# Layer 0's experts on gathered rows of the chosen pairs, after a routing of all batches

## The chip, the cores and the metric

One core of one Trainium2 chip runs the whole program in one launch. The metric is the device time of an execution in microseconds (us), the median of 3 runs. The engines are TensorE (PE in the profile; PEld is its weight load), VectorE (DVE), ScalarE (ACT), GpSimd (POOL) and SyncE (SP), which here only issues DMAs. Each runs its own queue in order and waits for the others by semaphores.

## The reference

Two transformer layers on x of shape (4, 512, 256). Each adds an attention part and a mixture of 8 experts, top 2, both on the layernorm of the same x:

```python
xn = _layernorm(x)
# L0 attention: q, k with rotary cos/sin, v; 16 heads of 16
memory = einsum('bhsd,bhse->bhde', elu(k) + 1, v)        # and softmax attention beside it
# L0 experts (F = 176)
top_w, sel = top_k(xn @ gate_w.T, 2); top_w = softmax(top_w)
h = silu(xn @ gate_proj[e].T) * (xn @ up_proj[e].T)      # for every expert e
out = sum_e tw[:, e] * (h @ down_proj[e].T)              # tw is zero but for the two chosen
x = x + attention + out
# L1: chunked linear attention with decay, experts with H = 512, top 2, the same way
```

## The kernel before

The program has three stages with a barrier between them. Stage one (`layer0_front`, tensors `a_...`) does layernorm, routing, the q/k/v projections, the memory matrix and the experts of layer 0. Stage two (`middle`, `b_...`) does the softmax attention of layer 0, and beside it, one batch behind, everything token-wise up to the routing of layer 1. Stage three (`layer1_main`, `d_...`) does the linear attention and the experts of layer 1; these already work on gathered rows.

Batches are 512 tokens. Matmuls on split operands stand in the helper `three` (L58 to L60): each product is hi x hi, hi x lo and lo x hi, so three matmuls.

In stage one the experts are computed **dense**: all 8 experts' hidden columns (8 x 176 = 1408) lie as 11 tiles of 128, and each tile is computed for all 512 tokens of a batch: `tile` on PE (L624) makes gate and up, 12 matmuls of 512 columns, into `psG`; ACT takes silu (L452), DVE multiplies by up (L528) and by the routing weight of its expert and token (L533, read from `cbc`, which SP loads as broadcast rows), ACT and POOL split the product in hi and lo (L455, L402), and `down` (L637) adds 12 matmuls of 256 columns into `psO`. There are 4 x 11 = 44 tiles. The front part of the next batch (layernorm, transposes, logits, routing, q/k projection with rotation, v, features, memory) stands as steps between the tiles, at places that a dictionary `steps` of every engine gives; PE runs two tiles ahead of `down` (`FAHEAD = 2`). The experts' sum is added to `xacc` in one DVE instruction a batch (L602).

In stage two the inner unit is a slot: four score matmuls, four more for row maxima of a later group (reduced by DVE, L1180), four exponentials on ACT (L1090), four value matmuls. Sixteen slots make a batch; the first batch has no token-wise work beside it. SP sends the maxima through memory (`send_max`, L918, L920) before a group of four slots may begin. At the end the tokens are ranked by expert (L1312 to L1377), which gives `put`, `take` and `expert`, the tables of stage three.

In stage three a block is 128 rows of one expert: POOL gathers them by an indirect DMA (L1767), PE transposes them, computes gate, up and down with the weights of the expert whose number PE loads into a register (`value_load`), and POOL scatters the result (L1776). There are `BLOCKS = 2*2048/128 + 7 = 39` blocks. At the end 32 DVE instructions multiply the returned rows by their weight and add them (L1901).

## Time and profile before

| | |
|---|---|
| median of 3 runs | 1087.56 us (1086.49 to 1091.96) |
| profiled execution | 1091.52 us, its span 1089.6 us |
| PE busy | 946.9 us (87% of the span) |
| DVE / ACT / POOL busy | 588.4 / 433.1 / 314.5 us |
| stage one, two, three (from the stretches' borders) | 299.4, 444.1, 346.1 us |

The span runs from the first to the last instruction; the execution has 1.9 us around it. Busy is time in which an engine works on an instruction; PE's matmuls are pipelined, so one that shows 0.39 us long is followed by the next after 0.23 us, and the distance of the starts is its price in a full queue. The end of stage one is the first instruction of stage two, 299.43 us.

### The profile page before, as it was taken

Reading aid. Unit: us, or ns where it says so; the run is one execution under the profiler, and the core shown is the slowest. Engines: PE = TensorE matmul, PEld = TensorE weight load, DVE = VectorE, ACT = ScalarE, POOL = GpSimd, SP = SyncE. Lnnn points to the kernel's source line nnn. Section 1 sums busy time; section 2 is a strip of 40 time slices with the busy share of each in tenths; the row PEclk is TensorE's granted clock in tenths of the full one; section 3 lists DMA queues with packets and bytes.
Section 4 is the critical chain, followed back from the end, with each engine's and each line's share of the span. In section 5 each row is a group of like instructions: output and inputs, shape, how many; then the busy total and the mean of one; then the engine's idle time right before and its main releaser. Section 6 shows DMA issues by size and latency. Waiting matters only on the chain. (4 is left out here: it accounts for less than half of the span.)

```text
span 1089.6 us, 16172 instructions
## 1 busy us (share of the span) xinstructions
PE 946.9 (87%) x5323; PEld 614.9 (56%) x5323; DVE 588.4 (54%) x1218; ACT 433.1 (40%) x663; POOL 314.5 (29%) x218
## 2 busy tenths in 40 slices
PE   3789999999858999998999988575999999999991
PEld 2678888888711234453445445463666666666660
DVE  4556655563268767647755741474443443443435
ACT  3335536353234554674576467041222222222220
POOL 3632515225233000211021020143333433433321
PEclk9999999999957989888998988786999999999995
DMA  5622414033051221133233112628873433433316
GB/s 200 217 96 60 165 58 144 19 97 126 1 166 58 92 79 60 59 107 131 92 101 118 55 59 99 161 106 298 241 234 86 122 104 88 118 106 97 98 43 236
DMA packets 149836, 125.26 MB, mean 115 GB/s; under 512 B 63232, under 2 KB 127504, under 8 KB 149776
## 3 DMA queue, kind: packets, MB, share of 16 engines
q1 hardware_dynamic: 146032, 114.25, 33.9%
q0 software_dynamic: 3744, 10.23, 2.7%
q8 instruction: 35, 0.57, 0.2%
q14 instruction: 25, 0.20, 0.1%
HBM read 85.56 MB, written 38.86 MB: 114 GB/s over the span
## 5 line engine op out<-in xcount | busy, mean ns | idle before, releaser
L1180 DVE TENSOR_REDUCE b_negmax<-b_psM 128x1 f32<-128x512 f32 x256 | 163.2, 683 | 82.1 <-PE b_psM L1408 79.1
L1090 ACT ACTIVATE b_probs<-b_psE 128x512 f32<-128x512 f32 x256 | 138.8, 595 | 122.8 <-PE b_psE L1426 121.8
L1408 PE MATMUL b_psM<-b_kst,b_qst 96*128 96x512 bf16 x256 | 98.9, 433 | 27.9 <-DVE b_negmax L1180 14.0
L1426 PE MATMUL b_psE<-b_qst,b_kst 98*128 98x512 bf16 x256 | 90.0, 412 | 15.1 <-ACT b_probs L1090 10.5
L402 POOL TENSOR_TENSOR a_hh<-a_h,a_hh 128x512 fp32r<-128x512 f32 x44 | 57.8, 1313 | 144.7 <-ACT a_hh L455 144.7
L1426 PEld LDWEIGHTS b_psE<-b_qst,b_kst 98*128 98x128 bf16 x256 | 21.0, 100 | 109.6 <-ACT b_probs L1090 54.1
L1435 PE MATMUL b_psV<-b_probs,b_vst 128*32 128x512 f32 x512 | 75.9, 667 | 3.1 <-ACT b_probs L1090 3.1
L1928 PE MATMUL d_psG<-d_w,d_xT 128*128 x156 | 76.5, 614 | 2.2 <-DVE d_xT L1827 1.9
L1776 POOL DMA_INDIRECT scratch_ys<-d_y,put x39 | 39.7, 1017 | 129.2 <-ACT d_y L1808 127.8
L1953 PE MATMUL d_psY<-d_w,d_hidden 128*128 x312 | 74.9, 383 | 0.0
L1936 PE MATMUL d_psU<-d_w,d_xT 128*128 x156 | 74.5, 600 | 0.0
L1408 PEld LDWEIGHTS b_psM<-b_kst,b_qst 96*128 96x128 bf16 x256 | 24.3, 100 | 83.6 <-DVE b_negmax L1180 60.1
L1837 DVE TENSOR_TENSOR d_probs<-d_ps,decay 128x512 f32<-128x512 f32 x64 | 43.6, 687 | 47.0 <-PE d_ps L1971 46.9
L528 DVE TENSOR_TENSOR a_h<-a_h,a_psG 128x512 f32<-128x512 f32 x44 | 30.2, 686 | 67.8 <-ACT a_h L452 67.8
L1953 PEld LDWEIGHTS d_psY<-d_w,d_hidden 128*128 128x128 f32 x312 | 57.6, 190 | 12.9 <-issue 6.8
L1808 ACT ACTIVATE d_y<-d_psY 128x256 f32<-128x256 f32 x39 | 14.9, 383 | 122.1 <-PE d_psY L1953 122.1
L1782 POOL TENSOR_TENSOR d_rs<-d_ss,d_neghalf 128x16 f32<-128x16 f32 x16 | 46.9, 2933 | 56.4 <-DVE d_ss L1866 56.4
L1032 POOL TENSOR_TENSOR b_combined<-b_both 128x256 f32<-128x256 f32 x16 | 11.6, 727 | 173.6 <-DVE b_both L1224 173.6
L1832 DVE TENSOR_TENSOR d_hidden<-d_hidden,d_psU 128x512 f32<-128x512 f32 x39 | 26.8, 687 | 59.8 <-PE d_psU L1936 59.8
L1796 ACT ACTIVATE d_hidden<-d_psG 128x512 f32<-128x512 f32 x39 | 23.3, 597 | 85.7 <-PE d_psG L1928 85.7
L455 ACT ACTIVATE a_hh<-a_h 128x512 fp32r<-128x512 f32 x44 | 27.8, 633 | 73.8 <-DVE a_h L533 73.8
L58 PE MATMUL a_psO<-a_wd,a_hh 128*128 128x256 f32 x176 | 50.1, 285 | 1.3 <-POOL a_hh L402 1.3
(314 smaller groups left out, 2125.5 us busy)
## 6 DMA issues: line engine op xcount, KB each, us to landing
scratch_parts<-a_part SPq DMA_DIRECT2D x12, 512.0 KB, 4.3
b_qst<-scratch_parts SPq DMA_DIRECT2D x96, 64.0 KB, 2.1
b_kst<-scratch_parts SPq DMA_DIRECT2D x96, 64.0 KB, 2.1
scratch_parts<-b_part SPq DMA_DIRECT2D x24, 256.0 KB, 3.4
chunk_qst<-scratch_parts SPq DMA_DIRECT2D x96, 64.0 KB, 2.9
chunk_kst<-scratch_parts SPq DMA_DIRECT2D x96, 64.0 KB, 2.2
a_cbc<-scratch_cT SPq DMA_DIRECT2D x16, 256.0 KB, 3.9
scratch_v<-a_v SPq DMA_DIRECT2D x4, 1024.0 KB, 4.4
```

The lines of the kernel that those rows point to most:

```text
L58: nc.tensor.matmul(out, ah, bh, start=start and i == 0, stop=False, skip_group_check=True)
L402: nc.gpsimd.tensor_tensor(hh[s % HSLOTS][1][:, :], h[s % 2][:, :], hh[s % HSLOTS][0][:, :].bitcast(F32), ALU.subtract).then_inc(lo_done, 1)
L1090: nc.scalar.activation(probs[k % PSLOTS][:, h, :], psE[h % 2][:, :], ACT.Exp, scale=float(HD) ** -0.5).then_inc(scores_used[h % 2], 1)
L1180: nc.vector.tensor_reduce(negmax[i][:, t, h:h + 1], psM[:, h % 2, :], AX_X, ALU.max, negate=True).then_inc(rows_used[h % 2], 1)
L1408: nc.tensor.matmul(psM[:, h % 2, :], qst[g][0:STACK, h, t * P:(t + 1) * P], kst[g][0:STACK, h, :], start=True, stop=True).then_inc(rows_re ...
L1426: nc.tensor.matmul(psE[h % 2][:, :], kst[g][0:STACKM, h, k * P:(k + 1) * P], qst[g][0:STACKM, h, :], start=True, stop=True).then_inc(score ...
L1435: mm = nc.tensor.matmul(psV[VW * h:VW * (h + 1), :], vst[g][:, k, VW * h:VW * (h + 1)], probs[k % PSLOTS][:, h, :], start=k == 0, stop=k = ...
L1782: nc.gpsimd.tensor_tensor(rs[:, :], ss[:, :], neghalf[:, :], ALU.pow).then_inc(rs_done, 1)
L1837: nc.vector.tensor_tensor(probs[g][:, :], (ps1 if g % 2 else ps0)[:, :], decay[:, HG * g:HG * g + HG, :].rearrange("p h c -> p (h c)"), AL ...
L1928: mm = nc.tensor.matmul(psG[:, :], xT[b % 2][:, k, :], weights(b, GATE + k * H1, H1), start=k == 0, stop=k == KT - 1)
L1936: mm = nc.tensor.matmul(psU[:, :], xT[b % 2][:, k, :], weights(b, UP + k * H1, H1), start=k == 0, stop=k == KT - 1)
L1953: mm = nc.tensor.matmul(psY[:, 0:D], hT[b % 2][:, k, :], weights(b, DOWN + k * D, D), start=k == 0, stop=k == HT1 - 1)
```

## The change

Stage one is written anew. Its order is a list that every engine walks (`front_order`):

1. The first part of all four batches (`prep`): layernorm, transposes, logits, top-2. The normalised rows are stored to memory (`xn0`). The transposed tokens of all batches stay in SBUF.
2. The ranking of all 4096 (token, expert) pairs: the class `Ranks`, the same operations that stage two has for layer 1, gives `put`, `take` and `expert`. Meanwhile POOL and ACT split the expert weights into hi and lo in 14 pieces (before: 5).
3. 39 blocks of 128 gathered rows. Each has `turn` (2 transposes), `gate` (6 matmuls of 352 columns: gate and up of one expert together), `turn_h` (2 transposes of the 176 hidden columns), `down` (6 matmuls of 256 columns), four ACT and three DVE operations, one gather and one scatter on POOL. The result is not weighted.
4. The projections, features and memory of the attention, in 10 steps a batch (`light`), 40 in all; the first stands before the ranking, the others between the blocks, about one a block.

In stage two, during the first batch of attention, the two returned rows of every token are multiplied by their weights and added: 32 DVE instructions, two a slot (`merge`). SP loads the rows of three batches into the memory of stage three's chunk buffers and those of the fourth when the first are merged.

```diff
+def front_order():
+    prep = [(0, 0), (1, 0), (0, 1), (2, 0), (0, 2), (1, 1), (0, 3), (3, 0), (1, 2), (2, 1), (0, 4), (1, 3), (2, 2), (3, 1),
+            (1, 4), (2, 3), (3, 2), (2, 4), (3, 3)]
+    order = [("prep", n, s) for n, s in prep]
+    lights = [("light", n, s) for n in range(BATCHES) for s in range(10)]
+    order += [lights[0], ("split", 0, 0), ("rank", 0, 0), ("prep", 3, 4), ("invert", 0, 0)]
+    order += [("turn", 0, 0), ("turn", 1, 0), ("gate", 0, 0), ("turn", 2, 0)]
+    rest, given, used = lights[1:], 0, 0
+    for b in range(BLOCKS + 1):
+        for kind, n in (("gate", b + 1), ("turn_h", b), ("down", b - 1), ("turn", b + 3)):
+            if 0 <= n < BLOCKS:
+                order.append((kind, n, 0))
+            used += 1
+            while given < min(len(rest) * used // (4 * (BLOCKS - 3)), len(rest)):
+                order.append(rest[given])
+                given += 1
+    return order
...
 @block.tensor
+            def gate(b, _):
+                owner[b] = pe.value_load(expert[0:1, b:b + 1], min_val=0, max_val=E - 1)
+                pe.wait_ge(xb_lo, b + 1)
...
+                if b >= 2:
+                    pe.wait_ge(mult_done, b - 1)
+                hi, lo = xb[b % 2]
+                pairs = []
+                for k in range(KT):
+                    wh, wl = (w[:, bass.ds(owner[b], 1), k * 2 * F0:(k + 1) * 2 * F0].rearrange("p a n -> p (a n)") for w in wgu)
+                    pairs.append((hi[:, k, :], lo[:, k, :], wh, wl))
+                three(nc, psG[:, b % 2, 0:2 * F0], pairs).then_inc(gate_ps, 1)
+            def turn_h(b, _):
+                pe.wait_ge(mult_done, b + 1)
+                if b:
+                    pe.wait_ge(hT_lo, b)
...
+            def down(b, _):
+                pe.wait_ge(hT_lo, b + 1)
...
+                if b:
+                    pe.wait_ge(y_done, b)
...
+            def light(n, s):
+                if s in (0, 2):
+                    project_qk(n, s // 2)
+                elif s == 4:
+                    project_v(n)
+                elif s == 6:
+                    turn_kf(n)
+                elif s == 8:
+                    memorise(n)
 @block.gpsimd
+            def turn(b, _):
+                if b + XSLOTS < BLOCKS:
+                    gather(b + XSLOTS)
+            def down(b, _):
+                pool.wait_ge(y_done, b + 1)
+                nc.gpsimd.indirect_dma_start(scratch["ys0"], bass.IndirectOffsetOnAxis(ap=put[:, b:b + 1], axis=0),
+                                             y[b % YSLOTS], None).then_inc(put_out[b % YSLOTS], 16)
 @block.scalar
+            def light(n, s):
+                if s == 2:
+                    exp_part(n, 0)
+                    first(n, 0)
+                elif s == 4:
+                    exp_part(n, 1)
+                elif s == 5:
+                    copy_v(n)
+                    first(n, 1)
...
 stage two, SP, before the first attention group
+            for n in range(BATCHES):
+                if n == BATCHES - 1:
+                    sp.wait_ge(merged, 2)
+                for i in range(2):
+                    sp.dma_start(back(n, i), scratch["ys0"][i * TOK + n * SEQ:i * TOK + (n + 1) * SEQ, :]
+                                 .rearrange("(t p) d -> p t d", p=P)).then_inc(back_in[n], 16)
 stage two, DVE, once a slot of the first batch
+            def merge(k):
+                for j in range(2 * k, 2 * k + 2):
+                    n, i, t = j // (2 * TILES), j // TILES % 2, j % TILES
+                    if j % (2 * TILES) == 0:
+                        dve.wait_ge(back_in[n], 32)
...
+                    last = nc.vector.scalar_tensor_tensor(x, back(n, i)[:, t, :], wts0[i][:, n * TILES + t:n * TILES + t + 1], x,
+                                                          ALU.mult, ALU.add)
```

PE between two units of expert work. Before, the end of a tile's `down` (`a_psO`), a step of the next batch and the start of the next tile:

```order
L58 MATMUL a_psO<-a_wd,a_hh 128x256
L59 MATMUL a_psO<-a_wd,a_hh 128x256
L60 MATMUL a_psO<-a_wd,a_hh 128x256
L651 ISA
L652 ISA
L655 MATMUL a_psT<-a_ident,a_xn 128x128 x8
L630 REGISTER_ALU
L58 MATMUL a_psG<-a_xTf,a_wg 128x512
L59 MATMUL a_psG<-a_xTf,a_wg 128x512
L60 MATMUL a_psG<-a_xTf,a_wg 128x512
```

Now the round of block 2 (`a_psH` is the transposed hidden, `a_psY` the block's result, `a_psT` the projection of q and k that stands as a step, `a_psG` the gate of the next block):

```order
L917 MATMUL a_psH<-a_ident,a_h 88x128 x2
L56 ISA
L56 MATMUL a_psY<-a_wd,a_hT 128x256
L57 REGISTER_ALU
...
L894 MATMUL a_psX<-a_ident,a_xg 128x128 x2
L56 MATMUL a_psT<-a_xT,a_wqk 128x512
...
L898 TENSOR_LOAD a_rk_expert
L898 ISA x2
L56 ISA
L56 MATMUL a_psG<-a_wgu,a_xb 128x352
```

The long runs of equal tiles are gone: a unit of expert work is 16 short matmuls and transposes, each with the weights picked by a number that PE loads for that block.

ACT around the exponential of the key and query features (`a_rot`), with the two table loads about it. Before it stands between two tiles of 512 columns (`a_h`, `a_hh`):

```order
L452 ACTIVATE a_h<-a_psG 128x512
L455 ACTIVATE a_hh<-a_h 128x512
L470 ISA
L471 ACT_TABLE_LOAD
L471 ACTIVATE a_rot<-a_rot 128x1024
L478 REGISTER_ALU
L479 ACTIVATE a_part<-a_qk 128x1024
L450 REGISTER_ALU
L452 ACT_TABLE_LOAD
L452 ACTIVATE a_h<-a_psG 128x512
```

Now it stands between a block's copies (`a_y` the result, `a_xb` the gathered rows, `a_hT` the hidden):

```order
L679 ACTIVATE a_hT<-a_psH 88x256
L686 ACTIVATE a_y<-a_psY 128x256
L666 ACTIVATE a_xb<-a_psX 128x256
L691 ACT_TABLE_LOAD
L691 ACTIVATE a_rot<-a_rot 128x1024
L697 ACTIVATE a_part<-a_qk 128x1024
L673 ACT_TABLE_LOAD
L673 ACTIVATE a_h<-a_psG 128x176
```

The step itself is unchanged; what stands before and behind it is a round of smaller instructions.

DVE in the first batch of stage two, a group of four slots. Before:

```order
L1180 TENSOR_REDUCE b_negmax<-b_psM 128x1 x4
L1203 COPY b_nmT<-b_psN 8x512
L1180 TENSOR_REDUCE b_negmax<-b_psM 128x1 x12
L1188 CAST b_nmparts<-b_negmax 128x4x4
L1190 TENSOR_TENSOR b_nmparts<-b_negmax,b_nmparts 128x4x4
L1210 COPY b_outT<-b_psV 128x512
```

Now:

```order
L1453 TENSOR_REDUCE b_negmax<-b_psM 128x1 x4
L1476 COPY b_nmT<-b_psN 8x512
L1680 SCALAR_TENSOR_TENSOR xacc<-held,wts,xacc 128x256 x2
...
L1453 TENSOR_REDUCE b_negmax<-b_psM 128x1 x4
L1680 SCALAR_TENSOR_TENSOR xacc<-held,wts,xacc 128x256 x2
L1461 CAST b_nmparts<-b_negmax 128x4x4
```

Each slot's four reductions are now followed by two merges.

## Rows read from the trace of the kernel before

**Rows 1.** Windows: length; PE, PEld, DVE, ACT, POOL busy (instructions); granted clock; DMA share; GB/s.
```profile
0.00:299.43 299.43, 261.12 (x1488) 227.15 (x1488) 162.31 (x326) 128.25 (x157) 117.82 (x74) 0.98 0.33 108
299.43:743.50 444.07, 372.77 (x1889) 175.85 (x1889) 279.32 (x578) 229.01 (x356) 71.70 (x49) 0.86 0.31 98
743.50:1089.60 346.10, 312.98 (x1946) 211.90 (x1946) 146.77 (x314) 75.88 (x150) 124.98 (x95) 0.95 0.48 143
308.00:331.00 23.00, 19.37 (x37) 3.55 (x36) 21.16 (x36) 9.18 (x25) 4.68 (x3) 0.50 0.58 162
336.00:395.80 59.80, 54.60 (x267) 13.33 (x268) 45.98 (x80) 32.54 (x60) 0.00 (x0) 0.95 0.22 68
```

**Rows 2.** Timeline, PE, inside a tile: start, duration, engine, line, operands, shape.
```profile
77.44 0.39 PE L58 MATMUL a_psG<-a_xTf,a_wg 128*128 128x512 f32 x1
77.67 0.40 PE L59 MATMUL a_psG<-a_xTf,a_wg 128*128 128x512 f32 x1
...
79.65 0.28 PE L59 MATMUL a_psO<-a_wd,a_hh 128*128 128x256 f32 x1
79.77 0.28 PE L60 MATMUL a_psO<-a_wd,a_hh 128*128 128x256 f32 x1
```

**Rows 3.** Timeline, the front part of the first batch, and POOL beside it.
```profile
13.15 1.02 ACT L462 ACTIVATE a_xT<-a_psT 128x1024 fp32r<-128x1024 f32 x1 [4.69 <-PE a_psT L655]
14.21 1.22 DVE L544 TENSOR_TENSOR a_xT<-a_psT,a_xT 128x1024 fp32r<-128x1024 f32 x1 [3.18 <-ACT a_xT L462]
...
17.84 6.12 POOL L433 TENSOR_TENSOR a_wg<-a_cbc,a_wg 128x2816 fp32r<-128x2816 f32 x1 [9.80 <-ACT a_wg L446]
...
20.26 0.35 PE L59 MATMUL a_psT<-a_wv,a_xT 128*128 128x8 f32 x1
20.47 0.35 PE L60 MATMUL a_psT<-a_wv,a_xT 128*128 128x8 f32 x1
...
21.57 2.42 DVE L153 TENSOR_TENSOR a_rt_gap<-a_rt_top 128x4 f32<-128x4 f32 x1
```

**Rows 4.** Timeline, DVE, first and last instruction of the ranking for layer 1.
```profile
716.45 0.15 DVE L1312 COPY b_counts<-b_psE 128x8 f32<-128x8 f32 x1
...
740.50 0.18 DVE L1377 TENSOR_SCALAR take<-put 128x40 uint32<-128x40 uint32 x1
```

**Rows 5.** Timeline, PE, stage three's second transposes and first gate (a register load between).
```profile
754.02 0.41 PE L1915 MATMUL d_psX<-ident,d_xg 128*128 128x128 f32 x2 [1.83 <-DVE d_xT L1827]
755.22 1.22 PE L1928 MATMUL d_psG<-d_w,d_xT 128*128 x1 [0.80 <-DVE d_xT L1827]
```

**Rows 6.** Timeline, POOL, two gathers in a row.
```profile
747.61 0.95 POOL L1767 DMA_INDIRECT d_xg<-scratch_xn,take  x1 [0.30 <-issue]
748.87 0.95 POOL L1767 DMA_INDIRECT d_xg<-scratch_xn,take  x1 [0.30 <-issue]
```

**Rows 7.** DMA issues: out<-in, queue, count, median us to landing.
```profile
d_xg<-scratch_xn,take POOLq DMA_INDIRECT x39, 3.6
```

**Rows 8.** Groups by line, stage one: busy us, mean ns; idle before, releaser.
```profile
L414 POOL TENSOR_TENSOR a_qk<-a_qk,a_part 128x1024 f32<-128x1024 f32 x8 | 19.7, 2457 | 7.6 <-DVE a_rot L583 7.6
L583 DVE SCALAR_TENSOR_TENSOR a_rot<-a_qk,a_rot 128x1024 f32<-128x1024 f32 x8 | 13.3, 1667 | 5.8 <-ACT a_rot L471 5.8
L452 ACT ACT_TABLE_LOAD x10 | 12.8, 1283 | 0.2
L471 ACT ACTIVATE a_rot<-a_rot 128x1024 f32<-128x1024 f32 x8 | 8.5, 1062 | 10.7 <-DVE a_rot L576 10.6
```

**Rows 9.** Timeline, stage two's first batch: ends of the first and fourth group; SP's maxima.
```profile
339.90 0.28 SPq L918 DMA_DIRECT2D scratch_max<-b_nmT  x1
...
351.89 0.69 DVE L1210 COPY b_outT<-b_psV 128x512 f32<-128x512 f32 x1
...
395.81 0.69 DVE L1210 COPY b_outT<-b_psV 128x512 f32<-128x512 f32 x1
```

**Rows 10.** One line's instructions: count, ns min/median/max, first and last start, shape.
```profile
L1901 DVE SCALAR_TENSOR_TENSOR xacc<-d_w,wts,xacc x32: 479/479/485, 1073.0 to 1085.8; 128x256 f32<-128x256 f32 x32
```

More of the change, by code:

```diff
@@ L302, in loop @@
-        def loop(eng, run):
-            with eng.Fori(0, BATCHES - 1) as b:
-                run(b, False)
-            run(BATCHES - 1, True)
-        def tiles(b, last, tile, steps):
-            for t in range(FT0):
-                before, behind = (() if last else steps.get((t, place), ()) for place in range(2))
-                for step in before:
-                    step(b + 1)
-                if not (last and t + FAHEAD >= FT0):
-                    tile(b, t + FAHEAD)
-                yield t
-                for step in behind:
-                    step(b + 1)
@@ L322, in start @@
-        def start(tile, steps):
-            for place in sorted(steps):
-                for step in steps[place]:
-                    step(0)
-            for t in range(FAHEAD if tile else 0):
-                tile(0, t)
-        def run_steps(eng, tile, steps):
-            def run(b, last):
-                for t in tiles(b, last, tile, steps):
-                    pass
-            return run
+        xmem = sb("xg", [P, XSLOTS * D])
+        xg = [xmem[:, i * D:(i + 1) * D] for i in range(XSLOTS)]
@@ L437, in _, with subtract @@
[L437 to L440 removed]
+            def subtract(i):
+                raw, hi, lo = piece(i)
+                pool.wait_ge(w_hi, i + 1)
+                if i:
+                    pool.wait_ge(w_lo, i)
+                nc.gpsimd.tensor_tensor(lo, raw, hi.bitcast(F32), ALU.subtract).then_inc(w_lo, 1)
@@ new lines, in split, with invert @@
+            def split(_, __):
+                for i in range(BATCHES, PIECES):
+                    subtract(i)
+                pool.wait_ge(w_lo, PIECES)
+            def invert(_, __):
+                pool.wait_ge(ranks.put_done, 3)
+                pool.wait_ge(xn_stored, 16 * BATCHES)
+                for b in range(XSLOTS):
+                    gather(b)
+            def turn(b, _):
[5 more added lines that the diff above has]
+                                             y[b % YSLOTS], None).then_inc(put_out[b % YSLOTS], 16)
@@ new lines, in rank, with invert, turn @@
+            def rank(_, __):
+                pe.wait_ge(routing.copied, BATCHES)
+                ranks.count(pe, psL)
+            def invert(_, __):
+                pe.wait_ge(ranks.routed, 12)
+                ranks.turn_over(pe, psL)
+            def turn(b, _):
+                s = b % XSLOTS
+                pe.wait_ge(gathered[s], 16 * (b // XSLOTS + 1))
+                if b == 1:
+                    pe.wait_ge(ranks.put_done, 3)
+                if b >= 2:
+                    pe.wait_ge(xb_lo, b - 1)
+                for k in range(KT):
+                    mm = nc.tensor.transpose(psX[b % 2][:, k * P:(k + 1) * P], xg[s][:, k * P:(k + 1) * P], ident[:, :])
+                mm.then_inc(x_ps, 1)
@@ L705, in memorise @@
                 pe.wait_ge(kf_copied, n + 1)
+                pe.wait_ge(ones, 2)
                 for k in range(KT):
@@ L870, in middle, with loop @@
         SLOTS = GROUPS * TILES
-        def loop(eng, attend, steps, ready=lambda: None):
+        def loop(eng, attend, steps, ready=lambda: None, first=lambda k: None):
             def batch(b, beside, last):
                 for g in range(GROUPS):
-                    attend(b, g, last, lambda k: [step(beside) for step in steps.get(TILES * g + k, ()) if beside is not None])
+                    attend(b, g, last, lambda k: first(TILES * g + k) if beside is None else
+                           [step(beside) for step in steps.get(TILES * g + k, ())])
             batch(0, None, False)
```

892 lines of the change are left out of this document (543 added, 349 removed).

## The prediction

> **What bounds the kernel now.** I read the windows by stage first [rows 1]. Stage one takes 299.43 us with PE busy for 261.12 at a granted clock of 0.98, that is 2.4 GHz nearly throughout, while DVE, ACT and POOL are busy for half of it or less. Stage one is bound by PE. In the first batch of stage two (the stretch from 336) three engines are close together: PE 54.60 and DVE 45.98 of 59.80 us. Then I read the timeline of PE inside a tile, for what a matmul costs in a full queue [rows 2]: 512 columns follow each other after 0.23 us, 256 columns after 0.12. A tile has 12 of either, 2.76 + 1.44 = 4.2 us, and 44 tiles are 185 us of the 299. That is what the change is after. The rest of stage one is the start, before tiles run, and the steps between them.
>
> The sum below is made against the profiled execution, 1091.5 us (span 1089.6). The median of the runs is 1087.6, so I take 4 us off at the end.
>
> **Stage one, up to the first block.** All four batches are routed before any expert runs. In the start of before, a batch passes through 8 transposes, a copy of 1.02 us on ACT, a difference of 1.22 on DVE and 24 small matmuls for the logits; these follow each other after 0.21 us, the clock being at 1.2 GHz there [rows 3]. That is 1.7 + 1.0 + 1.2 + 5.1 = 9.0 us, and as one batch's logits keep PE from the next one's transposes, the four come nearly one after the other. The first batch's logits end at 21 us as before; three more at 9.6 with the waits bring 50, the last top-2 gives 52. On PE the first q/k projection (12 matmuls at 0.43, the 1.2 GHz price of 512 columns) stands before the ranking: 55.5, and 17 counting matmuls: 57.5. The ranking itself is the chain that stage two has for layer 1: from 716.45 to 740.68, 24.2 us [rows 4]. Then a gather, 1.26 to issue [rows 6], 3.6 to landing [rows 7], and two copies: the first block's gate starts at **88 us**.
>
> The ranking's 24.2 us hold waits for POOL. One is in [rows 3]: a DVE instruction on 4 numbers lasts 2.42 us and ends when POOL's subtraction of 6.12 us, which began at 17.84, ends. In the change POOL still has nine or ten pieces to subtract then (6.12 us for 2816 columns, so 1.5 to 2.3 each, some 18 in all), about as much as it was busy beside the old chain. I keep 24; without such waits it would be 15, with more of them 32, so the block phase starts between 78 and 97.
>
> **Stage one, the 39 blocks.** Two floors. PE: a block has 6 matmuls of 352 columns (between 0.12 and 0.23, I take 0.16), 6 of 256 at 0.12 and 4 transposes at 0.12: 2.16 us, 39 times 84. A batch's attention steps are 24 matmuls of 512 columns, 24 of 256 and 16 short ones: 5.5 + 2.9 + 1.9 = 10.3, four times 41, of which 3 came before: 38. Together 122 us. New is a register load before each gate. Its bounds are in [rows 5]: 1.20 us lie between the start of two transposes and the gate behind them, 0.24 of it theirs, so up to 0.96 us where PE has nothing queued, and nothing where it has. I take 0.3, near the lower end since the blocks mostly leave work queued: 12 us (bounds 0 and 37). The Trainium skill gives such a load a floor of about 0.6 us (DMA: Bandwidth & Descriptors, Latency and other measured facts); by that alone, never hidden, it would be 23 us instead of 12.
>
> POOL: a gather and a scatter at 1.26 each [rows 6], 39 times 98 us, and 16 subtractions of the split at 2.46 [rows 8] are 39: 137 us. POOL, not PE, is the higher floor: 3.5 us a block.
>
> Neither floor will be reached, since the queues are in order and a block's chain has only one round of slack (`turn_h` needs the hidden of the gate one round earlier). Before, `FAHEAD` gave two tiles, 8.4 us. The step with the exponential costs ACT a wait of 10.7/8 = 1.3 for DVE, a table load of 1.28, 1.06 for itself, a copy of as much, and 1.28 to load the silu table back [rows 8]: 6.0 us, once a batch, and 4.9 once more without the copy. Against a round of 3.3 that leaves PE 2.7 and 1.6 idle. `turn_kf` waits for a DVE product of the same step (1.67, rows 8) behind the copy of the gathered rows: 2.7. So 7 us a batch, 28 in all. Rounds without a step, and the filling and emptying, cost about 6. Sum: 122 + 12 + 28 + 6 = **168 us**, 4.3 a block. Bounds: 137 (POOL's floor) and 205 (each wait twice as long, and the load never hidden).
>
> The end needs a last scatter and its landing and the barrier, 5 us. Stage two starts at 88 + 168 + 5 = 261 instead of 299.4: **38 us less** (between 8 more and 79 less). The removed row loads of the weights (`cbc`), POOL's 44 subtractions and `L602` were all beside PE and give nothing of their own.
>
> **Stage two.** Two merges a slot are 32 instructions, issued every 12.8/31 = 0.41 us [rows 10]: 13.2 us. A slot of the first batch lasts (395.81 - 351.89)/12 = 3.66 us [rows 9], and DVE idles (59.80 - 45.98)/16.3 = 0.85 us in each [rows 1]. The two merges want 0.83. They fit only if every gap is usable, and part of the gaps is waiting for PE, who in turn waits for the reductions. Between 0 and 13.2 I take 7. What is queued behind the merges are the next reductions, and PE's row matmuls wait for these.
>
> SP now waits for the first two `merged`, at the end of slot four, before it may send the maxima of the second group; before, these left at 339.90, 12 us before they were needed. The next group's scores then start some 4.5 us late (0 to 6). The first merge waits for rows whose load can't leave before the stage begins: 2 us (0 to 4). Together **13 us more** (1 to 24). Stage three is untouched, but for line numbers.
>
> Sum: 1091.5 - 38 + 13 = 1066.5, and for the median 4 less: **1063 us**.
>
> **The rivals.**
> *All hidden but POOL.* ACT's long steps fall into slack and the blocks run at POOL's 137 us: 31 less again, 1032. For it: stage three runs the same block scheme with PE busy 312.98 of 346.10 [rows 1]. Against: its blocks last over 7 us of PE each, so POOL and ACT have twice the slack there.
> *No change.* The block phase takes 193 us (4.95 a block), and start and merges eat the gain: 1083 to 1092. It needs twice my waits.
> *The clock, slower.* PE waits in each round, the clock falls to 1.2 GHz and stays: the 122 us of PE work become 244, the load and the filling stay, 262 us, and the time is 1063 + 94 = 1157; with half of the phase at that clock, 61 more, some 1120. It decides from about 25 us of extra PE time on. For it: in the stretch from 308 to 331, where PE waits for DVE after each pair of matmuls, the granted clock is 0.50. Against it: from 336 on PE waits too, in smaller pieces, and has 0.95 [rows 1]. The Trainium skill has a rule that speaks for it (TensorE: Matmul & The Clock Gate, A second HAM failure mode: psum-queue depth-cycling): frequent short idles between groups of matmuls make the clock swing. I trust the 0.95 more, since a slot of attention is about as long as a block.
>
> **Chances.** Forecast (1048 to 1078) 0.52; all hidden 0.22; no change 0.10; clock 0.16. A measurement of this kernel can tell 0.5%, 5.4 us, from no change. Faster by more: the first two and a little of the third, 0.77; within it 0.06; slower 0.17. The range 1030 to 1108 takes in most of the fast rival and the mild part of the slow one; the forecast's own is 1048 to 1078.
>
> **What would show it.** Right: the first gate of 352 columns at 78 to 97 us; starts of gates 4.3 us apart on average, the longest gaps at the exponentials and before `turn_kf`; stage two's first instruction near 261; slots of the first batch at 4.1 us with a gap once after the fourth; granted clock over 0.85 in the blocks. Wrong: a clock near 0.5 there, gates over 5 us apart, POOL's indirect DMAs much longer than 1 us, or a ranking over 32 us.

## The result, and the profile after

Over six runs each, on the same chips, the changed kernel takes 1079.6 us (median, 1074.2 to 1081.6) and the kernel before 1090.7 (1086.5 to 1095.0): ratio 0.9887, 95% interval 0.9855 to 0.992. It is faster, by 11 us or 1.1%. Forecast were 24.5 us, 2.3%; the time lies inside the range of 1030 to 1108, but the gain is just under half of what was forecast.

The profiled execution took 1074.2 us, 17.3 less than that of before. By stages, from one profile of each (here the border of stage three is its first instruction, 744.05 us before and 726.53 after, so stage two of before is 0.5 us longer than in [rows 1]):

| us | before | forecast | after |
|---|---|---|---|
| first gate of a block | | 88 | 89.2 |
| blocks, first gate to last `down` | | 168 | 176.9 |
| from there to stage two | | 5 | 9.6 |
| stage one | 299.4 | 261 | 275.7 |
| stage two | 444.6 | 457 | 450.9 |
| stage three | 345.6 | unchanged | 345.8 |
| profiled execution | 1091.5 | 1066.5 | 1074.2 |
| median less profiled | | -4 | +5.4 |

The windows by stage, then the block phase, the first batch of stage two, and the rest of it; the columns are those of [rows 1]:

```profile
0.00:275.66 275.66, 182.64 (x1089) 167.40 (x1089) 148.70 (x372) 118.71 (x228) 152.13 (x121) 0.87 0.37 120
275.66:726.53 450.87, 371.00 (x1889) 171.60 (x1889) 290.78 (x610) 229.00 (x356) 71.71 (x49) 0.86 0.34 106
726.53:1072.30 345.77, 313.23 (x1946) 212.00 (x1946) 146.74 (x314) 75.86 (x150) 124.73 (x95) 0.95 0.53 144
89.20:266.10 176.90, 144.42 (x896) 133.70 (x896) 90.58 (x188) 100.47 (x203) 114.27 (x91) 0.89 0.37 126
275.66:387.55 111.89, 82.67 (x311) 18.73 (x312) 82.58 (x150) 45.48 (x91) 17.63 (x12) 0.72 0.41 124
387.55:726.53 338.98, 288.33 (x1580) 152.87 (x1578) 208.20 (x461) 183.52 (x266) 54.08 (x37) 0.90 0.31 99
```

Stage one's granted clock was 0.98 in [rows 1]; in the block phase it is 0.89. PE is busy for 144.4 us there and idle for 32.5. At the pitches of a full queue at 2.4 GHz (the distance from one start to the next) the same matmuls cost 118: 234 gates at 0.16, 234 downs at 0.12, 76 pairs of transposes at 0.14, 84 of 512 columns at 0.23, 96 of 256 at 0.12 and 11 for the rest. So 26 us of "busy" lie above these pitches. Most of them stand in the timeline behind the longest kind of wait (PE; the bracket is the idle time before):

```profile
201.32 0.39 PE L894 MATMUL a_psX<-a_ident,a_xg 128*128 128x128 f32 x2
206.70 1.94 PE L964 MATMUL a_psT<-a_ident,a_rot 128*128 128x128 f32 x8 [4.99 <-DVE a_rot L830]
208.29 0.64 PE L56 MATMUL a_psG<-a_wgu,a_xb 128*128 x1
208.73 0.50 PE L57 MATMUL a_psG<-a_wgu,a_xb 128*128 x1
209.02 0.50 PE L58 MATMUL a_psG<-a_wgu,a_xb 128*128 x1
...
212.33 0.32 PE L57 MATMUL a_psG<-a_wgu,a_xb 128*128 x1
212.49 0.32 PE L58 MATMUL a_psG<-a_wgu,a_xb 128*128 x1
```

Before the wait PE ran at 2.4 GHz; behind five idle microseconds a gate matmul follows the last after 0.29 us, at 212 us after 0.16 again. The granted clock is 0.50 in 37.4 of the 176.9 us. The first 3.3 of them are left from before the phase; the rest are seven stretches, and each begins within a wait of 1.4 to 5.0 us or at most 1.1 us behind one. What the matmuls in all of them cost above the 2.4 GHz pitches is 16 us. The other 10 or 11 us stand at full clock. Some 4 are the matmul before an idle time, whose recorded length is more than its pitch, so a bit of waiting is booked as busy. Some 6 are the first matmul of a group, also in a full queue: the first gate takes 0.25 us instead of 0.16 and the first `down` 0.20 instead of 0.12. The waits themselves (engine, line, what released it: total, times, longest):

```profile
PE a_psT L964 <- DVE a_rot L830: 17.6, 4, 5.0
PE a_psT L56 <- DVE a_rot L815: 10.6, 8, 1.9
PE a_psH L917 <- DVE a_hT L800: 2.8, 4, 1.2
PE a_psY L56 <- ACT a_y L686: 0.9, 2, 0.7
PE a_psG L56 <- issue: 0.7, 2, 0.4
```

The last row would show the register loads before the gates: 0.7 us, where 12 were forecast.

In stage two the answer to [rows 9] is, on SP and DVE:

```profile
312.06 21.57 SPq L1210 DMA_DIRECT2D held<-scratch_ys  x8
333.74 0.34 SPq L1184 DMA_DIRECT2D scratch_max<-b_nmT  x1
337.77 0.26 SPq L1186 DMA_DIRECT2D b_qst<-scratch_max  x1
...
315.97 0.41 DVE L1476 COPY b_nmT<-b_psN 8x512 bf16<-8x512 bf16 x1 [0.75 <-PE b_psN L1707]
319.32 0.88 DVE L1680 SCALAR_TENSOR_TENSOR xacc<-held,wts,xacc 128x256 f32<-128x256 f32 x2 [2.94 <-DMA held<-scratch_ys]
...
332.88 0.68 DVE L1483 COPY b_outT<-b_psV 128x512 f32<-128x512 f32 x1
357.91 0.68 DVE L1483 COPY b_outT<-b_psV 128x512 f32<-128x512 f32 x1
```

The maxima lie ready at 316.4 us and leave at 333.7. Eight row loads stand ahead of them in SP's queue, but their issue takes little: six are out by 316.9, and then SP stands until 332.7, for the second `merged`. From the store of the maxima to SP's next issue it is 4.0 us, where it was 1.3 before (339.90 to 341.19); the last two row loads left right ahead of it and landed at 336.6 and 338.0. PE waits for what the maxima release:

```profile
339.34 1.03 PE L1718 MATMUL b_psE<-b_qst,b_kst 98*128 98x512 bf16 x2 [6.89 <-DMA b_qst<-scratch_max]
```

This wait is paid twice too: from 334.9 to 348.5 us the granted clock is 0.50. It was also 0.50 from 321.2 to 328.0, where the first group's reductions had kept PE idle for 2.0 us. Between the ends of the first and the second group are 25.0 us instead of 14.6; the third and fourth take 14.8 as against 14.6. The first batch costs 111.9 instead of 96.4 us, 15.5 more.

And the end of stage one on POOL, the last scatters and stage two's first instruction:

```profile
265.42 0.97 POOL L608 DMA_INDIRECT scratch_ys<-a_y,a_rk_put  x1 [0.82 <-ACT a_y L686]
267.05 0.97 POOL L608 DMA_INDIRECT scratch_ys<-a_y,a_rk_put  x1 [0.67 <-ACT a_y L686]
275.66 1.80 POOL L1337 MEMSET b_kst<- 2x2048 bf16 x1 [7.64 <-POOLq L72]
```

The scatter has landed 2.4 us after its issue, at 269.5. Then nothing runs and no byte moves for 6 us. Before, stage two began 1.1 us after DVE's last instruction.

### The profile page after: what moved, and what is told of

The parts are those of the page before. It is cut to its first block and busy times, and to the rows that moved or that the text cites. A ratio compares the mean times of both kernels' runs of the same rounds, so it can differ in the third digit from the quotient of the medians.

```text
span 1072.3 us, 15783 instructions
## 1 busy us (share of the span) xinstructions
PE 866.9 (81%) x4924; PEld 551.0 (51%) x4924; DVE 586.2 (55%) x1296; ACT 423.6 (40%) x734; POOL 348.6 (33%) x265
## 5 line engine op out<-in xcount | busy, mean ns | idle before, releaser
L1363 ACT ACTIVATE b_probs<-b_psE 128x512 f32<-128x512 f32 x256 | 138.8, 595 | 130.9 <-PE b_psE L1718 130.3
L1700 PE MATMUL b_psM<-b_kst,b_qst 96*128 96x512 bf16 x256 | 101.8, 443 | 37.5 <-DMA b_vst<-scratch_v 18.2
L608 POOL DMA_INDIRECT scratch_ys<-a_y,a_rk_put x39 | 43.2, 1108 | 43.8 <-ACT a_y L686 38.6
L581 POOL DMA_INDIRECT a_xg<-scratch_xn,a_rk_take x39 | 41.3, 1059 | 27.9 <-issue 19.3
L2057 POOL DMA_INDIRECT d_xg<-scratch_xn,take x39 | 38.1, 977 | 21.4 <-issue 11.0
L2218 PEld LDWEIGHTS d_psG<-d_w,d_xT 128*128 128x128 f32 x156 | 27.3, 194 | 23.2 <-issue 23.1
```

The costliest lines, as they stand in the source:

```text
L581: nc.gpsimd.indirect_dma_start(xg[s], None, scratch["xn0"].rearrange("b s d -> (b s) d"), bass.IndirectOffsetOnAxis(ap=take[:, b:b + 1], a ...
L608: nc.gpsimd.indirect_dma_start(scratch["ys0"], bass.IndirectOffsetOnAxis(ap=put[:, b:b + 1], axis=0), y[b % YSLOTS], None).then_inc(put_ou ...
L1363: nc.scalar.activation(probs[k % PSLOTS][:, h, :], psE[h % 2][:, :], ACT.Exp, scale=float(HD) ** -0.5).then_inc(scores_used[h % 2], 1)
L1700: nc.tensor.matmul(psM[:, h % 2, :], qst[g][0:STACK, h, t * P:(t + 1) * P], kst[g][0:STACK, h, :], start=True, stop=True).then_inc(rows_re ...
L2218: mm = nc.tensor.matmul(psG[:, :], xT[b % 2][:, k, :], weights(b, GATE + k * H1, H1), start=k == 0, stop=k == KT - 1)
```

## The experiments

Ratios are against the kernel before on the same chip. "Blocks" is first gate to last `down`, as in the table.

### Both kernels once more

> The changed kernel once more, for the spread of each stage between two profiles. If the profiled execution of the change (1074.2 us) was only a lucky one, this profile lies at 1077 to 1082 us, and the 3 to 7 us more stand in stage two, whose later three batches took 274 us in the changed kernel and 283 in the kernel before on the same code: then the 8.5 us were chance. If they belong to the change, stage two's later batches take 274 us again and the total stays within 2 us of 1074. Stage one is expected within 3 us of 275.7 by both.

> The kernel before once more, for the spread between two profiles. Stage one 299 us within 1; the later twelve groups of stage two vary in steps of 1.3 to 1.7 us in every profile of the changed kernel (12 groups and the end 331 to 345 us); if that holds for the code of before too, this profile differs from the first by 2 to 8 us there and nowhere else.

The change: 1079.3 us, ratio 0.989 (0.984 to 0.994), this profile 1084.2, above the 1077 to 1082 that I had given it. Blocks 176.8 us, end 9.6, first batch of stage two 112.2: all repeat to 0.3 us. Two runs below whose stage one is untouched have 177.0 (late_rows) and 178.7 (no_merge) for the blocks, so one profile of them is good to some 2 us. What moved is the rest of stage two, 347.0 instead of 339.0. The kernel before, profiled again (1093.5): first batch 96.9, and the rest

```profile
400.60:746.10 345.50, 294.19 (x1581) 159.31 (x1582) 207.43 (x460) 183.86 (x266) 53.52 (x37) 0.88 0.31 97
```

where the first profile had 348.2. Over the 18 profiles of this study this stretch lasts 339.0 to 348.2 us, whatever was edited, and the two profiles first compared are the ends of that range. The 9 us that the change seems to gain there are chance, and more than cover the difference between 17 us by profiles and 11 by medians. That stage one repeats within 3 us held for the change (277.6) but was too narrow for the kernel before (303.7; I had said within 1).

### Stage two: SP's order, and the merges

`late_rows`:

```diff
             load(0, 3)
-            for n in range(BATCHES):
-                if n == BATCHES - 1:
-                    sp.wait_ge(merged, 2)
-                (load the returned rows of batch n)
+            load_back(0)
 in attend, behind send_max:
+                if isinstance(b, int) and b == 0 and g < 3:
+                    if g == 2:
+                        sp.wait_ge(merged, 2)
+                    load_back(g + 1)
```

> SP sends the second group's maxima right after the rows of the first batch; the rows of the second to fourth batch are loaded behind the sends of the next groups. Queue theory (the 21.6 us in which SP's queue issues the row loads and waits for the first merges hold back the maxima, 333.7 us in the changed kernel where they were ready at 316.4): the first four groups of stage two end at 88 to 92 us after its start instead of 96.4 plus 15.5, that is 103 instead of 112, the second group takes 15 us instead of 25, and the time falls by 8 to 11 us. Rival (the merges themselves hold DVE and so PE): the second group stays above 20 us and the time falls by less than 3 us.

1065.0 us, ratio 0.979 (0.974 to 0.984), 1.0% below the change. In time that is 14 us below it on the same chip, where 8 to 11 were expected. On SP the maxima now leave soon:

```profile
313.47 1.06 SPq L1208 DMA_DIRECT2D held<-scratch_ys  x2
317.58 0.29 SPq L1184 DMA_DIRECT2D scratch_max<-b_nmT  x1
319.34 0.26 SPq L1186 DMA_DIRECT2D b_qst<-scratch_max  x1
319.64 0.93 SPq L1208 DMA_DIRECT2D held<-scratch_ys  x2
```

The second group takes 14.8 us, and from 319.8 us to the end of the batch the granted clock is 1.00. The first batch takes 98.3 us. That is 13.6 us less than in the change. I expected 88 to 92 in one place and 103 in another for it; the first was a slip, and the second too cautious, since the first group gained as well (53.8 instead of 57.2).

`no_merge` leaves the row loads and the merges out:

```diff
             def merge(k):
+                return
```

> Leaves out the load of the returned rows and the 32 merges of stage two, so layer 0's experts are not added. It prices all of what stage two pays. Queue theory: the first batch falls back to the 96.4 us of the kernel before, 15 us less, and with late_rows at 10 less, the merges on DVE are worth 5 or less. Rival (merges are dear on DVE, as the prediction's 7 us and its bound of 13.2): this one lies over 8 us below late_rows.

1069.1 us, ratio 0.981. Its first batch takes 96.8 us, as before (96.4). So loads and merges, well placed, cost 98.3 - 96.8 = 1.5 us; the queue order cost 13.6, between these two profiles. The eleven profiles with the change's order of SP have 106.4 to 112.2 us for this batch, whatever was edited in stage one, and the four with the late loads 98.0 to 99.9: the order costs 6.5 to 14 us. The total lies above that of late_rows only by the rest of stage two (348.1 against 343.0).

### The blocks: where PE waits, and what the wait costs

`turn_later`, PE's and ACT's steps on the key features one step later (ACT's copy, from step 7 to 8, is not shown):

```diff
-                elif s == 6:
+                elif s == 7:
                     turn_kf(n)
-                elif s == 8:
+                elif s == 9:
                     memorise(n)
```

> PE transposes the key features one step later (and ACT's copy and PE's memory matmuls too), so DVE's product has a round more. In the changed kernel PE waits 17.6 us in four places for it, and each time its clock is low for some 5 to 10 us behind. Theory that the waits bring the low clock: these four waits shrink under 1.5 us each, the granted clock of the blocks rises from 0.89 to 0.93 or more, and stage one is 14 to 24 us shorter. First rival (the clock falls whatever PE does): the waits go, the clock stays at 0.89, stage one is 10 to 16 us shorter. Second rival (ACT with its table loads and copies is the limit, the wait only moves): stage one less than 5 us shorter, and PE waits as long for ACT's copies of the blocks.

1078.6 us, ratio 0.989: nothing. Blocks 178.6 us. The waits of PE:

```profile
PE a_psT L56 <- DVE a_rot L814: 10.7, 8, 1.9
PE a_psT L971 <- ACT a_xn L716: 8.1, 4, 2.5
PE a_psH L916 <- DVE a_hT L799: 4.7, 6, 1.8
PE a_psT L963 <- DVE a_rot L829: 3.5, 3, 1.7
```

The wait for L829 (L830 in the change) fell from 17.6 to 3.5 us and came back before the memory matmuls and before `turn_h`. The second rival holds in that the wait only moves; that ACT's table loads are behind it is not what exp_as_copy shows below.

`feature_early`, the product itself earlier:

```diff
-                elif s in (5, 6):
-                    feature(n, s - 5)
+                elif s == 5:
+                    feature(n, 0)
+                    feature(n, 1)
```

> DVE makes both feature products one step earlier, behind each other, instead of the second behind the block's work of the next step. In the changed kernel the exponential that it needs ended at 197.7 us, DVE began the product at 204.7 and PE waited until 206.7. Theory that DVE's order makes this wait: the four waits of 4 to 5 us (17.6 together) fall to 2 to 3 each, under 11 together, and the blocks take 7 to 12 us less than 177, a part of it from the clock. Rival (it moves elsewhere, as in turn_later): blocks 174 to 179, with more waits for DVE's other products (L790, L800).

1069.9 us, ratio 0.980 (0.977 to 0.984). The window of the blocks:

```profile
89.70:258.30 168.60, 142.54 (x896) 129.76 (x896) 85.81 (x188) 99.61 (x203) 116.25 (x91) 0.93 0.39 133
```

and PE's wait is down from 17.6 to 7.3:

```profile
PE a_psT L965 <- DVE a_rot L830: 7.3, 4, 2.8
```

The exponential had long been done; what held the product was DVE's own order, as DVE's rows of the change show, where it stands behind the block's differences (L800, L790), which wait for ACT:

```profile
201.99 1.22 DVE L830 SCALAR_TENSOR_TENSOR a_rot<-a_qk,a_rot 128x1024 f32<-128x1024 f32 x1
203.85 0.42 DVE L800 TENSOR_TENSOR a_hT<-a_psH,a_hT 88x256 fp32r<-88x256 f32 x1 [0.65 <-ACT a_hT L679]
204.39 0.42 DVE L790 TENSOR_TENSOR a_xb<-a_psX,a_xb 128x256 fp32r<-128x256 f32 x1
204.73 1.82 DVE L830 SCALAR_TENSOR_TENSOR a_rot<-a_qk,a_rot 128x1024 f32<-128x1024 f32 x1
```

`fill` leaves the waits and gives PE something to do in them:

```diff
                 pe.wait_ge(v_copied, n + 1)
+                for _ in range(32):
+                    nc.tensor.matmul(psT[:, 0, 0:D], wv[0][:, 0, 0:P], xT[n][0][:, 0, 0:D], start=True, stop=True,
+                                     skip_group_check=True)
                 pe.wait_ge(features, 2 * n + 2)
```

> At the four places where PE waits 4 to 5 us for DVE's product it first runs 32 matmuls of 256 columns into a buffer that is free there (3.8 us of work with no use, behind ACT's copy of v, so inside the wait). Nothing else is changed. Theory that PE's waits bring the low clock: the pitches at double length behind these places go, the sum of slow pitches falls from 16 us to 10 or less, the granted clock of the blocks rises to 0.92 or more and the blocks are 4 to 8 us shorter, though PE has 15 us more to do. Rival (the clock falls by itself, or by the sum of the work): slow pitches stay at 14 to 18 us, the blocks take 176 to 180.

1071.9 us, ratio 0.981 (0.978 to 0.984). The block phase, then the same place as above:

```profile
91.00:262.60 171.60, 154.17 (x1024) 141.53 (x1024) 90.63 (x188) 100.42 (x203) 116.10 (x91) 0.95 0.39 130
```

```profile
200.99 4.08 PE L961 MATMUL a_psT<-a_xT,a_wv 128*128 128x256 f32 x32 [0.96 <-ACT a_v L710]
204.97 1.09 PE L967 MATMUL a_psT<-a_ident,a_rot 128*128 128x128 f32 x8
205.84 0.42 PE L56 MATMUL a_psG<-a_wgu,a_xb 128*128 x1
206.10 0.32 PE L57 MATMUL a_psG<-a_wgu,a_xb 128*128 x1
206.26 0.32 PE L58 MATMUL a_psG<-a_wgu,a_xb 128*128 x1
```

With 128 useless matmuls more (15.4 us) the blocks are 5.3 us shorter. Take these 15.4 from PE's 154.2: the useful part took 138.8 instead of 144.4. The eight transposes take 1.09 instead of 1.94 us and the gates follow each other after 0.16 instead of 0.29. So the idle wait brings the low clock here; this is shown. The stretches at a granted clock of 0.50 shrink from 37.4 to 16.7 us, and what the matmuls in them cost above the 2.4 GHz pitches falls from 16 to 7, under the 10 that were set. Three stretches are left; they begin at 107.7, 193.1 and 234.0 us, within or just behind the waits of 1.7 to 1.9 us before the v projections, which were not filled.

`exp_together` and `exp_as_copy`:

```diff
 exp_together, ACT
                 if s == 2:
-                    exp_part(n, 0)
                     first(n, 0)
                 elif s == 4:
+                    exp_part(n, 0)
                     exp_part(n, 1)
 exp_as_copy, ACT
-                nc.scalar.activation(rot[:, half, :], rot[:, half, :], ACT.Exp).then_inc(exp_done, 1)
+                nc.scalar.activation(rot[:, half, :], rot[:, half, :], ACT.Copy).then_inc(exp_done, 1)
```

> Both exponentials of a batch stand in one step, so ACT loads 4 exponential and 4 silu tables less (8 times 1.28 us, 10.2 us of ACT). In turn_later the four waits for DVE's product (17.6 us) came back as 17 us at other places, so ACT's chain is suspected. Theory that ACT's chain of table loads and copies sets these rounds: the blocks take 8 to 12 us less than 177, and the four waits of 4 to 5 us fall under 4. Rival (the wait is the chain PE, DVE, ACT, DVE of a projection, in which a table load is hidden behind DVE's 2.8 us): the blocks stay within 3 us of 177.

> The exponentials of stage one are replaced by copies of the same size: no table is loaded between the blocks (16 loads, 20.5 us of ACT, go; the features are wrong). If ACT's chain sets the rounds: blocks 15 to 22 us shorter, and if the low clock comes from the waits, the granted clock of the blocks rises from 0.89 to 0.93 or more and the pitches at double length (16 us of them) halve. If the chain of a projection sets them: under 5 us, the clock unchanged.

1070.1 us, ratio 0.980 (0.977 to 0.982), blocks 165.7; and 1066.8 us, ratio 0.974, blocks 169.7. The windows of the block phase, first the joined exponentials, then the copies:

```profile
91.50:257.20 165.70, 137.84 (x896) 128.43 (x896) 90.58 (x188) 91.48 (x195) 114.62 (x91) 0.92 0.40 135
```

```profile
89.20:258.90 169.70, 141.57 (x895) 131.34 (x896) 91.41 (x188) 80.05 (x187) 117.38 (x91) 0.90 0.39 132
```

Neither fits its theory. The joined exponentials gained the 11 us, but not where I said: the four long waits stayed (17.7). All of PE's idle time fell by 4.6 us (32.5 to 27.9) and its busy time, on the same matmuls, by 6.6. Without any table load but the first (exp_as_copy) the idle time is the same 28.1, and the blocks are 4 us longer by busy time alone. So a table load as such is mostly hidden, and the two differ by where the clock fell. Why it fell less in the first stays open; in a second profile of the joined form (below) the blocks take 167.1.

`fixed_owner`:

```diff
-                owner[b] = pe.value_load(expert[0:1, b:b + 1], min_val=0, max_val=E - 1)
+                owner[b] = b // 5
```

> Each block's expert number is fixed as block / 5 in the program, so PE loads no register (the wrong weights are used). The prediction held 12 us for these loads; the trace of the changed kernel shows 0.7 us of waits before gates that nothing else explains. By the trace: blocks within 2 us of 177. By the prediction: 12 us less. A third way: the loads delay PE's queue where no wait is shown, at the first matmul behind a wait: 3 to 8 us less.

Blocks 176.3 us against 176.8 to 178.7 in the four profiles of the same stage with the loads: the 39 loads cost 0.5 to 2.4 us together. The ratio (0.985, 0.982 to 0.988) is nominally lower, by stage two's first batch (108.5) and the rest of it.

`lights_last`, the steps of the attention all behind the last block:

```diff
-            while given < min(len(rest) * used // (4 * (BLOCKS - 3)), len(rest)):
+            while False:
...
+    order += rest[given:]
     return order
```

> All attention steps but the first stand behind the last block, so the 39 blocks run alone, and the steps alone after them. PE's work of a block is 2.0 to 2.2 us, POOL's gather and scatter 2.5. If POOL is the floor of a block, as the prediction has it: 2.5 to 2.7 us a block, 98 to 105 in all. If one round of slack is too short for the chain through ACT and DVE: 3 us or more, over 117. If neither, PE sets it: 80 to 88. The steps alone should take over 35 us a batch, 140 in all, so the time is 60 us or more above the changed kernel: the mixing hides them.

1093.6 us. The windows of the blocks alone, then of the steps alone:

```profile
89.80:187.00 97.20, 91.66 (x620) 83.88 (x620) 44.86 (x119) 49.58 (x155) 71.09 (x73) 0.97 0.31 100
187.00:285.80 98.80, 63.23 (x279) 51.87 (x277) 46.68 (x70) 33.48 (x34) 38.46 (x20) 0.79 0.33 120
```

2.49 us a block, where two indirect DMAs at POOL's pitch of 1.26 make 2.52: the price per block that the prediction's floor rests on fits. POOL's idle time there is 18.9 us of "issue", the 0.3 us that lie between any two of its indirect DMAs, and only 7.5 us of waits for others. But PE is busy for 91.7 of the 97.2 us too, at a granted clock of 0.97, where 39 times the prediction's 2.16 is 84; and no third quantity was varied. One round of slack is enough for a block alone. The steps took 98.8 us, not over 140, and the whole took 19 more than the change's profile, in one run, not 60: mixing the two hides only 196 - 177 = 19 us.

### The end of the stage

`tail` spreads the steps so that the last seven stand behind or between the last two blocks, and `pool_end` also gives POOL's last subtraction to DVE:

```diff
-            while given < min(len(rest) * used // (4 * (BLOCKS - 3)), len(rest)):
+            while given < min(len(rest) * used // (4 * (BLOCKS + 5)), len(rest)):
...
+    order += rest[given:]
 pool_end, DVE (and POOL's own step 8 only for n < BATCHES - 1)
+                elif s == 8 and n == BATCHES - 1:
+                    nc.vector.tensor_tensor(parts[2][:, half, :], qk[:, half, :], parts[1][:, half, :], ...)
```

> The attention steps are spread wider, so that the last seven stand behind the last two blocks, and the last scatter leaves some 10 us before the stage ends. In the changed kernel 9.6 us lie between the last matmuls of a block and stage two, 6.6 us of them behind the last bytes of the last scatter; in the kernel before 1.1 us lie between DVE's last instruction and stage two. Theory (POOL's queue takes long after a scatter, before the barrier opens): from the last instruction of any engine to stage two under 3 us. Rival (the barrier itself is longer now, for the many semaphores that it clears or for the code that it loads): 6 us again from the last instruction or store to stage two. The time as a whole may rise by up to 10 us, since the last steps lie bare.

> As tail (last seven attention steps behind the last blocks), and POOL's last subtraction goes to DVE, so that POOL's last instruction ends 3 to 5 us before the last store leaves. In all kernels of this shape stage two starts 7.65 us after POOL's last instruction, whether that is a scatter or a subtraction. If POOL's queue holds the barrier for 7.6 us after its last instruction: stage two starts 7.65 us after POOL's last again, so 3 to 4 us after the last store's issue. If it is the barrier or SP's wait: 7.3 us after the last store's issue again, as in tail, and over 10 us after POOL's last instruction.

tail: 1072.7 us, ratio 0.980 (0.977 to 0.983); stage two starts at 270.2, 5.5 earlier, so the wider spacing gains where I feared a loss. pool_end: 1066.7 us in one run. POOL in tail, then in pool_end:

```profile
260.40 2.12 POOL L622 TENSOR_TENSOR a_part<-a_qk,a_part 128x1024 bf16<-128x1024 f32 x1 [1.17 <-ACT a_part L703]
270.18 3.54 POOL L1338 MEMSET b_kst<- 2x2048 bf16 x2 [7.66 <-POOLq L72]
```

```profile
259.94 2.13 POOL L616 TENSOR_TENSOR a_qk<-a_qk,a_part 128x1024 f32<-128x1024 f32 x1
269.73 1.80 POOL L1344 MEMSET b_kst<- 2x2048 bf16 x1 [7.65 <-POOLq L72]
```

In pool_end the last store leaves 4.9 us before stage two, in tail 7.3; but from the end of POOL's last instruction it is 7.65 in both, as in every kernel here with the new stage one (7.64 to 7.66), whether that instruction is a scatter or a subtraction. POOL holds the barrier. The theory that I gave tail, a POOL that is slow just behind a scatter, fails with it. In the kernel before, whose stage one has no indirect DMA, stage two started 4.15 us after POOL's last instruction, and 1.1 after DVE's. That the indirect DMAs make the difference, and not something else in the new stage, is argued, not shown.

### Together

```diff
 late_rows_exp_together = late_rows + exp_together
 best2 = late_rows + exp_together + feature_early + tail
 best3 = best2 + POOL's last subtraction on DVE + fill with 12 matmuls instead of 32
```

> Both edits that gained by themselves: the late row loads (ratio 0.979 against the kernel before) and the joined exponentials (0.9795), where the change alone has 0.989. One sits in stage two, the other in stage one, so they should add: 1.0 + 1.0 per cent below 0.989, ratio 0.966 to 0.973. Rival (both only shift the phase of the clock in stage two, whose later groups vary by 10 us from run to run): 0.975 to 0.980. Blocks 165 to 167 us, first batch of stage two 98 us.

> late_rows, exp_together, feature_early and tail's wider spacing together. If their gains add in the blocks (11 for the joined exponentials, 6 for the spacing, 8 for the products) and 14 in stage two: stage two starts at 250 to 256 us and the ratio to the kernel before is 0.950 to 0.960. If the waits are shared and count once: stage two at 259 to 264, ratio 0.961 to 0.967, no better than late_rows_exp_together's 0.966.

> best2 with POOL's last subtraction on DVE, and 12 matmuls without use (1.4 us) where PE waits for the products. POOL theory: stage two starts 7.65 us after POOL's last instruction and 2 us or more earlier than in best2. Clock theory: granted clock of the blocks 0.01 to 0.03 higher than in best2. Together 2 to 6 us less than best2; rival: within 2 us of it, since the waits are already short.

Ratios 0.966 (0.963 to 0.970; 1056.6 us), 0.960 (0.957 to 0.963; 1046.2) and 0.956 (0.953 to 0.960; 1042.7 us): each beats both kernels, best3 the kernel before by 4.4%. Stage two starts at 256.8 in best2, a little behind the 250 to 256 of gains that add, and at 251.5 in best3, 7.65 us behind POOL in both; the difference of their ratios is within the intervals. The window of best3's block phase, which has some 24 useful matmuls fewer inside, since these stand behind the last block:

```profile
89.10:235.40 146.30, 133.83 (x908) 123.33 (x908) 85.55 (x186) 85.36 (x191) 104.29 (x87) 0.98 0.39 131
```

Idle time is 14.8 us in best2 and 12.5 in best3, the clock 0.96 and 0.98: less waiting, a higher clock, twice paid.

## Why the prediction was right and wrong, by its steps

**Start.** The first gate of 352 columns was forecast at 88 us and stands at 89.2 (91.2 in the second profile). The ranking takes 26.3 us (56.65 to 82.96), where 24 were taken from stage two of before: that chain, with its waits for POOL, was the right measure.

**PE's work in the blocks, the step that failed.** "Together 122 us" is right as a count of matmuls times their pitch at 2.4 GHz in a full queue (118 by the count above), and it was taken as the time that PE spends. It spent 144.4. Of the 26 us more, 16 are the low clock. The prediction had this mechanism as its rival "the clock, slower", but as a matter of all or half of the phase, and priced the forecast itself at no slow clock at all, on the 0.95 of [rows 1]. The measured clock of 0.89 is 21% of the phase at 1.2 GHz, in pieces behind the waits. The forecast's own 28 us of waits should have carried such a price. The other 10 us were in no rival: units cut this short cost more than count times pitch at full clock too, as the first matmuls of the groups in fill show (205.84 to 206.10 us, 0.26 instead of 0.16). The Trainium skill (TensorE: Matmul & The Clock Gate, A second HAM failure mode: psum-queue depth-cycling), cited for the rival, speaks of frequent short idles between groups of matmuls, with which the clock swings. The trace agrees in kind, with seven falls of the clock in the phase, and fill shows the cause.

**Register loads, over-priced.** 12 us were held; fixed_owner measures 0.5 to 2.4. The row used as bound showed PE with nothing queued, and in the blocks PE mostly has work queued: only 0.7 us of waits stand before the gates. The Trainium skill gives such a load a floor of about 0.6 us (DMA: Bandwidth & Descriptors, Latency and other measured facts). The estimate from it, 23 us if never hidden, is not what came: here the loads are hidden nearly in full.

**Waits, right in size.** 28 and 6 for filling were forecast, 32.5 came. That the sum fits is luck, since the split was off. The features' product cost 4.4 each time, 17.6 in all, not 2.7 and 11, because of DVE's order. The exponential's steps were given 2.7 and 1.6 a batch, 17 in all; without exponentials and their table loads (exp_as_copy) the idle time falls by 4.4 only. And 10.6 us, where a projection waits until DVE has rotated the last one (L815), were in no term. That the first could be mended (17.6 to 7.3) was not seen.

So the blocks: 122 - 4 + 26 for work, 12 - 11 for loads, 34 - 2 for waits, 177 instead of 168. The errors in work and in loads have opposite signs and hide each other in part.

**The end.** 5 us were held for the last scatter and a barrier as short as the one before; POOL needs 7.65 from its last instruction alone. It took 9.6, so 4.6 us more.

**Stage two, right in sum, wrong in its parts.** 13 forecast, 15.5 measured (10 to 16 over the profiles with this order of SP). The merges were given 7 and cost at most 1.5 with their loads: DVE's gaps took them nearly whole. SP's order was given 4.5, with an upper bound of 6, and with the waits for the first rows given 2, it cost 13.6. The wait was the one foreseen, SP standing for `merged`, and PE stood 6.9 us for it. What was left out is the low clock behind it, to 348.5 us, and the first group, 57.2 us instead of late_rows' 53.8, with its own low stretch. How much of the 13.6 each of these is was not varied alone.

**The median.** 4 us were taken off because the median of three runs lay 4 below the profiled execution. Over all runs on the same chips as the change's, the median of before is 1090.7, 0.8 below its profile, so there was next to nothing to take off. That is 3 us of the miss in time. It does not touch the forecast gain, which is counted from the lower median of before, 1087.6.

Together, in gain: 25 us forecast, less 15 in stage one and 2.5 in stage two's first batch, leave some 8. The medians show 11; the 3 us between are within what the rest of stage two varies by itself.

## What to carry to other kernels

When long uniform matmul runs are cut into short units with waits between, price each wait twice: once as idle time and once as the matmuls behind it at half clock. Add the longer first matmul of every group. Work without use inside a wait that can't be removed can pay. Loads that are put "beside" a stage, and the waits that guard them, must be followed through the queue of the engine that issues them, up to the next message that somebody waits for: what SP stood for here (15.8 us, for `merged`) held the maxima behind it. And before two profiles are compared by stage, the same code should be looked at in both: stretches that no edit touched differed by 9 us here.

## What the hardware showed that I had not expected

- With 15.4 us of matmuls added, the phase became 5.3 us shorter (fill), since the eight transposes behind a filled wait took 1.09 instead of 1.94 us.
- A stage whose POOL queue has indirect DMAs ends 7.64 to 7.66 us after POOL's last instruction, in 16 profiles, whatever that instruction is; before the change 4.15 us were enough.
- A register load for dynamic weights, 39 times, costs 0.5 to 2.4 us in all when PE has work queued.
- The same matmuls cost more than their pitch at full clock too: the first gate of a group 0.25 us instead of 0.16, the first `down` 0.20 instead of 0.12, some 6 us over 39 blocks.
